# Cross attention's mask moved from a TensorE matmul to a VectorE addition, in a one-core perceiver layer

## The chip, the cores and the metric

The kernel runs on one core of a Trainium2 chip. The metric is the device time of one execution in microseconds; the median of several executions is given. "The profile" is one execution recorded by the hardware profiler, with its trace of every instruction.

## What is computed

One layer on 16 sequences of 64 tokens of 256 numbers: cross attention over a context, self attention, and a mixture of experts, each added to x. The change touches the cross attention only:

```python
# x: (16, 64, 256), ctx: (16, 1601, 256), seg_id: (16, 64), here always 0..127; H=16, HD=128, R=64
kv_c = ctx @ W_kvc ; q_c = layernorm(x) @ W_dq
scores = (q_nope . k_nope + rope(q_rope) . rope(k_rope)) / sqrt(HD + R)
good = (k_ids <= seg_id) & (k_ids >= seg_id - 8)
scores = where(good, scores, -1e30)
attn = softmax(scores)                 # over the context positions
x = x + (attn @ v) @ W_o
x = x + self_attention(layernorm(x))   # 16 heads of 16, causal
x = x + moe(x)                         # 8 experts, top 2, and 2 shared ones
```

A token sees at most nine context positions, all of them within the first 128 where the segment numbers are below 128. So the kernel reads 128 context positions, and has a general path over all 1601 behind a flag that these inputs leave unset.

## The kernel before

The 1024 tokens are 8 tiles of 128, and a tile is two sequences ("blocks" b = 0 and 1) of 64 tokens. Cross attention takes tile after tile: `body(0)`, `body(1)`, a hardware loop over tiles 2 to 6, and `last_body(7)`, which already mixes in the first steps of self attention. Each engine has its own `body`, written out by hand, and semaphores join them. Every `body(i)` also makes the queries and keys of tile i + 1.

The scores of a block are 8 slices of 128 rows (two heads of 64 tokens) by 128 context positions, in two PSUM banks of four slices (banks 4 and 5 for b = 0, 6 and 7 for b = 1). They hold the negated scores, since keys are scaled by a negative number, so softmax takes the minimum.

TensorE, `body` (L1559): transpose of x (`xT`), `scores(i, 0)`, `values(i-1, 1)`, `qc`, `kv`, `y_lat`, `y_rope` of the next tile, `probs_T(i, 0)`, `scores(i, 1)`, `project(i-1)`, `k_T`, `q_T` in two halves (L1359, shown under the helper's line L1320 like every transpose), `values(i, 0)`, `probs_T(i, 1)`. `scores_work` (L1362) begins each bank with one matmul (L1364) that spreads a table of masks over the rows: `sel` picks the row of the block and `win` holds 1e30 where a position is not seen. Four score matmuls (L1368; each f32 matmul runs as two passes in the trace) are summed on top of it.

VectorE, `body` (L698): `maxima(i, 0)` (L643: per bank one `tensor_reduce` from PSUM, L648, then `top_ready`), the copy of the compressed query (L627), `divided(i, 0)` (L652, L653), keys rotated (L603 to L623), `front_rotate` (L609 to L611, which waits for `y_rope`), `maxima(i, 1)`, `front_rotated` (L636, signals `qrope`), `divided(i, 1)`, `front_qt` (L640), the next norm, the residual. In `body(0)` two copies of folded weights (L714) stand behind L636.

ScalarE, `body` (L1152): `exps(i, 0)` (L1097: eight times an exponential of 128x128 with its row sum, each with an accumulator read behind it), `kv_out` (L1086), `kv_raw_out` (L1071 and L1072, signals `kv_raw`, for which `y_rope` waits), `lat_out`, `pt_out` (L1104), `exps(i, 1)`, `k_out` (L1081, signals `kT_done`, for which the second half of `q_T` waits), `qt_hi_out` (L1090), two copies.

GpSimd (L503 to L508) makes `win` [128, 8, 128] once: subtract, square, compare. TensorE waits for it before `body(0)` (L1654). `link` on VectorE and GpSimd makes the engine wait for its own last instruction; in the loop VectorE counts K = 8 such steps per tile.

Of the kernel before, what the change touches and what calls it, by code (L numbers as in the profile page):

```python
# [92 lines left out]
def build(nc, dram):  # L93
    with ExitStack() as ctx:
        def sb(name, shape, dt=F32):
            return ctx.enter_context(nc.sbuf_tensor(name, shape, dt))
# [19 lines left out]
        keypos = packed(consts_a, PACK_A, "keypos")  # L116
        seg_i = sb("seg_i", [P, NT], I32)
        tril = packed(consts_b, PACK_B, "tril")
        hmask = packed(consts_b, PACK_B, "hmask")
        half = sb("half", [P, NT])  # L120
        seg = sb("seg", [P, NT])

# [4 lines left out]
        def carve(store):  # L127
# [102 lines left out]
        xT_all = sb("xT_all", [P, NT, KT, P])  # L230
        b_down = sb("b_down", [P, IC * D])
        b_up = [w_shared[:, 0, 0:GU], x_up[:]]
        b_dn = [w_shared[:, 0, GU:], b_down[:]]
# [49 lines left out]
            yrope_ps yrope_used qrope krope kT_ps kT_done qt_lo_ps qt_lo qt_hi_ps qt_hi kvx  # L283
            s_ps top_ready exp_done p_done pt_ps pt_done ut_ps ut_done proj_ps x2_done ones_set
            bxn bT_ps bxT_done bq_ps bqm bkv_ps bk_done bv_done bs_ps bs_used bmax bsub bp_done bpt_ps
# [7 lines left out]
         yrope_ps, yrope_used, qrope, krope, kT_ps, kT_done, qt_lo_ps, qt_lo, qt_hi_ps, qt_hi, kvx,  # L293
         s_ps, top_ready, exp_done, p_done, pt_ps, pt_done, ut_ps, ut_done, proj_ps, x2_done, ones_set,
         bxn, bT_ps, bxT_done, bq_ps, bqm, bkv_ps, bk_done, bv_done, bs_ps, bs_used, bmax, bsub, bp_done, bpt_ps,
# [37 lines left out]
        def general(eng, tile, first=None, clear=None):  # L333

            eng.wait_ge(far_ready, 1)
            flag = eng.value_load(far_i[0:1, 0:1], min_val=0, max_val=1)
            with eng.If(flag > 0):
                eng.wait_ge(x0_in, 16)
                eng.wait_ge(x_in, 16)
                eng.wait_ge(wv_in, 16)  # L340
                eng.wait_ge(qlat, 1)
                eng.wait_ge(krope, 1)
                eng.wait_ge(qrope, 1)
                eng.wait_ge(win_ready, 1)
# [16 lines left out]
        def _(sp):  # L361
# [114 lines left out]
        def _(pool):  # L476
            steps = [0]

            def link(ins):
                steps[0] += 1  # L480
                ins.then_inc(pool_step, 1)
                pool.wait_ge(pool_step, steps[0])
# [17 lines left out]
            for i in range(2):  # L500
# [3 lines left out]
            pool.wait_ge(seg_moved, 1)  # L504
            link(pool.tensor_tensor(dist, keypos[:].unsqueeze(1).to_broadcast([P, NT, P]),
                                    seg[:].unsqueeze(2).to_broadcast([P, NT, P]), ALU.subtract))
            link(pool.tensor_tensor(dist, dist, dist, ALU.mult))
            pool.tensor_scalar(win[:], dist, (LOOKBACK / 2) ** 2, -NEG, ALU.is_gt, ALU.mult).then_inc(win_ready, 1)  # L508

# [53 lines left out]
        def _(dve):  # L563
# [78 lines left out]

            def maxima(i, b):  # L643
                s = scores_at(b)
                for g in range(2):
                    n = slice(4 * g, 4 * g + 4)
                    dve.wait_ge(s_ps, 2 * TB * i + 2 * b + g + 1)
                    dve.tensor_reduce(neg_top[:, b, n], s[:, n], AX.X, ALU.min).then_inc(top_ready, 1)  # L648

# [35 lines left out]
            def last_body(i, link_):  # L685
                normed(0, 5, xn, bT_ps, bxn, 0)
                maxima(i, 0)
                divided(i, 0, link_)
                b_queries(0)
                maxima(i, 1)  # L690
                normed(1, 7, xn, bT_ps, bxn, 1)
                divided(i, 1, link_)
                residual(i - 1, link_)
                b_maximum(0)
                b_queries(1)
                normed(2, 9, xn, bT_ps, bxn, 2)

            def body(i, link_, behind, more):  # L698
                maxima(i, 0)
                query_compressed(i + 1)  # L700
                if more:
                    link_(dve.bn_stats(bn[:], x_sb[:, i + 2, :]))
                divided(i, 0, link_)
                if more:
                    link_(dve.bn_aggr(mv1[:], bn[:]))
                    dve.tensor_tensor(mv[:, i + 2, :], mv1[:], eps[:], ALU.add).then_inc(mv_ready, 1)
                front_k(i + 1, link_)
                front_rotate(i + 1)
                maxima(i, 1)
# [15 lines left out]
            link(dve.tensor_copy(seg[:], seg_i[:]))  # L725
            dve.tensor_scalar(far[:, 0:NT], seg[:], float(P - 1), None, ALU.is_gt)
            link(dve.tensor_scalar(far[:, NT:2 * NT], seg[:], 0.0, None, ALU.is_lt))
            dve.tensor_reduce(far_n[:], far[:], AX.X, ALU.max).then_inc(flag_set, 1)
# [72 lines left out]
            front_qt(0)  # L801
            dve.wait_ge(x_in, 16)
            body(0, link, False, True)
            body(1, link, True, True)
            base = steps[0]
            K = 8
            with dve.Fori(2, NT - 2) as i:
# [224 lines left out]
        def _(act):  # L1032
# [59 lines left out]
            def exps(i, b, groups=(0, 1)):  # L1092
                s = ps[:, 4 + 2 * b:6 + 2 * b, :].rearrange("p r (h t) -> p (r h) t", t=P)
                for g in groups:
                    act.wait_ge(top_ready, 2 * TB * i + 2 * b + g + 1)
                    for n in range(4 * g, 4 * g + 4):
                        last = act.activation(Pb[:, b, n, :], s[:, n, :], ACT.Exp, scale=-1.0,  # L1097
                                              bias=neg_top[:, b, n:n + 1], accum_out=sums[:, b, n:n + 1])
                    if g:
                        last.then_inc(exp_done, 1)  # L1100
# [217 lines left out]
        def _(pe):  # L1318
# [42 lines left out]

            def scores_work(b, half_, window):  # L1362
                at = ps[:, 4 + 2 * b + half_, :]
                pe.matmul(at.rearrange("p (n k) -> p n k", k=P), sel[:, b, :], window.unsqueeze(1).to_broadcast([P, 4, P]),  # L1364
                          start=True, stop=False)
                for n in range(4):
                    h = 2 * (4 * half_ + n)
                    last = pe.matmul(at[:, n * P:(n + 1) * P], QT[:, b, h:h + 2, :], KTb[:, b, :], start=False, stop=n == 3)  # L1368
                return last
# [560 lines left out]
def laid_out(inputs):  # L1930

    a = {k: np.asarray(v) for k, v in inputs.items()}
    g = lambda n: a["L0_xattn_" + n]
    s = lambda n: a["L0_attn_" + n]
    rows = lambda w: w.reshape(KT, P, -1).transpose(1, 0, 2)
    heads = lambda w, n: w.reshape(n, H, HD).transpose(2, 1, 0)

    def expert(gate, up, down):
# [44 lines left out]
```

## Time and profile before

| what | value |
|---|---|
| median of 3 runs | 513.69 us (513.13 to 515.97) |
| the profiled execution | 514.32 us, of it 512.5 us span |
| TensorE / weight loads busy | 97% / 70% |
| VectorE / ScalarE / GpSimd busy | 48% / 36% / 13% |
| cross attention | from about 23 us to 181 us |

Shares of the whole span mix three stages. The question for this change is what each engine waits for within one tile of cross attention, which the timeline of one tile shows. In the timeline a line has the start, the duration from the first to the last of the merged instructions, and in brackets the idle time before and who ended it. Instructions overlap on an engine: where one follows another without a wait, the distance of two starts (the step) is shorter than the duration.

### The profile page before, as it was taken

How to read it: one execution, taken by the hardware profiler on the slowest of the kernel's cores; microseconds unless marked ns; L12 is line 12 of the kernel's file. 1: busy time of each engine (PE TensorE's matmuls, PEld its weight loads, DVE VectorE, ACT ScalarE, POOL GpSimd, SP SyncE). 2: the span in 40 equal slices, each digit the busy share in tenths (PEclk: the TensorE clock that was granted, in tenths of full speed). 3: DMA queues.
4: the chain of work that ended last, by engine and by line, in shares of the span. 5: the costliest groups of instructions: out<-in, count | busy, mean ns of one | idle time of the engine just before them, and what ended most of it. 6: DMA issues, size and time to landing. Idle time of an engine off the chain costs nothing.

```text
span 512.5 us, 10574 instructions
## 1 busy us (share of the span) xinstructions
PE 496.6 (97%) x3878; PEld 361.1 (70%) x3878; DVE 247.4 (48%) x547; ACT 185.1 (36%) x533; POOL 67.6 (13%) x74
## 2 busy tenths in 40 slices
PE   8799999999999999998999998999999999999997
PEld 7566876876887788886788885555555555556886
DVE  2585776776776678888552221212212222222334
ACT  2267566666667544444411111212212112111110
POOL 6200000000000122232006500000000000000650
PEclk9999999999999999999999999999999999999999
DMA  7830000002990019300704272687877878852341
GB/s 224 300 113 22 0 22 20 0 20 82 369 388 2 2 62 428 128 0 1 277 35 133 73 263 60 262 299 258 313 278 268 321 265 280 306 198 83 86 120 41
DMA packets 24887, 82.05 MB, mean 160 GB/s; under 512 B 2928, under 2 KB 16560, under 8 KB 20880
## 3 DMA queue, kind: packets, MB, share of 16 engines
q1 hardware_dynamic: 21824, 73.30, 39.6%
q0 software_dynamic: 1536, 4.20, 2.6%
q10 hardware_dynamic: 1488, 4.00, 2.1%
q8 instruction: 28, 0.46, 0.3%
q14 instruction: 11, 0.09, 0.1%
HBM read 73.10 MB, written 8.39 MB: 159 GB/s over the span
## 4 chain that ended last, share of the span: by engine, by line
PE 87%; DVE 6%; issue 3%; DMA 1%; ACT 1%; SPq 0%; POOL 0%; DVEq 0%; POOLq 0%
PE ps L1817 17%; PE ps L1725 13%; PE ps L1320 12%; PE ps L1841 9%; PE ps L1737 6%; PE ps L1399 5%; PE ps L1349 5%; PE ps L1368 5%; PE ps L1491 3%; PE ps L1387 3%; DMA w_shared<-in_w_uqk 1%; PE ps L1341 1%; PE ps L1501 1%; PE ps L1681 1%; PE ps L1364 1%
## 5 line engine op out<-in xcount | busy, mean ns | idle before, releaser
L1817 PE MATMUL ps<-w_routed,xnT 128*64 x320 | 93.8, 436 | 1.6 <-DVE x_sb L973 1.6
L1725 PE MATMUL ps<-xT_all,w_shared 128*128 128x256 f32 x320 | 75.6, 380 | 0.0
L1817 PEld LDWEIGHTS ps<-w_routed,xnT 128*64 128x64 f32 x320 | 42.0, 137 | 38.4 <-issue 27.2
L1725 PEld LDWEIGHTS ps<-xT_all,w_shared 128*128 128x128 f32 x320 | 60.3, 190 | 8.4 <-issue 0.4
L1097 ACT ACTIVATE w_routed<-ps,neg_top 128x128 f32<-128x128 f32 x128 | 45.1, 379 | 15.9 <-DVE neg_top L648 15.9
L1841 PE MATMUL ps<-w_routed,hidT 128*64 x200 | 47.4, 384 | 0.0
L1817 PE MATMUL ps<-w_shared,xnT 128*64 128x384 f32 (+1 forms) x160 | 46.9, 436 | 0.0
L1817 PE MATMUL ps<-x_up,xnT 128*64 128x384 f32 (+1 forms) x160 | 46.9, 436 | 0.0
L1320 PEld LDWEIGHTS ps<-consts_a,w_routed 128*128 128x128 f32 x336 | 37.2, 141 | 13.5 <-issue 10.4
L1289 ACT COPY hidT<-ps 128x384 f32<-128x384 f32 x20 | 9.6, 479 | 100.7 <-PE ps L1320 100.7
L1262 ACT ACTIVATE sil<-ps 128x256 f32<-128x256 f32 x40 | 15.4, 384 | 84.3 <-PE ps L1725 84.2
L1320 PE MATMUL ps<-consts_a,w_routed 128*128 128x128 f32 x336 | 44.3, 276 | 1.1 <-DVE w_routed L835 0.5
L1841 PEld LDWEIGHTS ps<-w_routed,hidT 128*64 128x64 f32 x200 | 25.8, 137 | 15.0 <-issue 3.3
L1368 PEld LDWEIGHTS ps<-hid,w_routed 128*128 128x128 f32 x256 | 33.6, 192 | 1.2
L967 DVE COPY hidT<-ps 128x256 f32<-128x256 f32 x20 | 8.5, 425 | 53.4 <-PE ps L1320 53.4
L1368 PE MATMUL ps<-hid,w_routed 128*128 128x128 f32 x256 | 33.7, 275 | 0.0
L558 POOL DMA_INDIRECT x_up<-y_slots,slot_i x8 | 8.0, 997 | 182.7 <-DVE hidT L880 180.5
L648 DVE TENSOR_REDUCE neg_top<-ps 128x4 f32<-128x512 f32 x32 | 22.0, 689 | 16.6 <-PE ps L1368 16.1
L497 POOL TENSOR_TENSOR rstd<-mv,half 128x1 f32 (+1 forms) x16 | 9.1, 567 | 156.8 <-DVE mv L578 95.9
L1349 PE MATMUL ps<-w_routed 96*128 96x512 f32 x64 | 28.9, 593 | 0.3 <-issue 0.3
L1399 PE MATMUL ps<-w_routed 128*128 128x256 f32 x128 | 28.9, 379 | 0.0
L1097 ACT ACTIVATION_READ_ACCUMULATOR w_routed<-ps,neg_top 128x1 f32 x128 | 27.9, 218 | 0.0
(180 smaller groups left out, 873.8 us busy)
## 6 DMA issues: line engine op xcount, KB each, us to landing
w_routed<-in_w_routed SPq DMA_DIRECT2D x8, 1920.0 KB, 14.2
x_up<-in_w_routed SPq DMA_DIRECT2D x10, 1280.0 KB, 5.8
w_shared<-in_w_routed SPq DMA_DIRECT2D x10, 1280.0 KB, 6.1
b_down<-in_w_routed SPq DMA_DIRECT2D x10, 640.0 KB, 5.6
w_shared<-in_w_routed SPq DMA_DIRECT2D x10, 640.0 KB, 5.1
w_shared<-in_w_shared SPq DMA_DIRECT2D x1, 3840.0 KB, 11.8
w_shared<-in_w_uvo ACTq DMA_DIRECT2D x1, 2560.0 KB, 12.7
x_slots<-sil SPq DMA_DIRECT2D x16, 160.0 KB, 2.2
```

Of the source, the lines that this page charges most:

```text
L648: dve.tensor_reduce(neg_top[:, b, n], s[:, n], AX.X, ALU.min).then_inc(top_ready, 1)
L1097: last = act.activation(Pb[:, b, n, :], s[:, n, :], ACT.Exp, scale=-1.0, bias=neg_top[:, b, n:n + 1], accum_out=sums[:, b, n:n + 1])
L1262: act.activation(sil_ring[m % 2], ps[:, UP_BANK[m], 0:D], ACT.Silu).then_inc(up_sil, 1)
L1320: return pe.transpose(out, src, ident[:])
L1349: last = pe.matmul(ps[:, 2 * part + c, :], qcT[:], w[:, c * 512:(c + 1) * 512], start=True, stop=True)
L1368: last = pe.matmul(at[:, n * P:(n + 1) * P], QT[:, b, h:h + 2, :], KTb[:, b, :], start=False, stop=n == 3)
L1387: last = pe.matmul(ps[KVC * h:KVC * h + KVC, 4 + 2 * b, :].rearrange("p (j t) -> p j t", t=P), kv_ext[:, b, 0:KVC], PT[:, b].rearrange("p ...
L1399: last = pe.matmul(ps[:, b, 0:D], UT[:, j, h, :], w_m[:, 2 * j + h, :], start=j == h == 0, stop=j == NP_ // 2 - 1 and h == 1)
L1725: last = pe.matmul(ps[:, UP_BANK[m], half_ * D:(half_ + 1) * D].rearrange("p (n t) -> p n t", n=2), w_shared[:, j, at:at + P], xT_all[:, i ...
L1737: last = pe.matmul(ps[:, Y_BANK[g][n], n * D:(n + 1) * D], hidT_ring[m % 4][:, n * P:(n + 1) * P], w_shared[:, PAIRS[g][0], GU + c * D:GU ...
L1817: last = pe.matmul(ps[rows, b, 0:hi - lo], xnT[:, k, rows], w, start=k == 0, stop=k == KT - 1)
L1841: last = pe.matmul(ps[rows, 6, 0:D], hidT[:, c, rows], w, start=c == 0, stop=c == IC - 1)
```

## The change

The mask is no longer part of the matmul group. Segment numbers come from the host three times side by side: as before, and for each block b its 64 numbers repeated over both halves of the 128 rows. GpSimd makes a table for each block (`spread`, bf16, [128, 2, 8, 128], in the buffer `b_down`), where it made one. VectorE adds the table to a bank of scores, PSUM to SBUF (`Pb`), waits for itself, and takes the minimum from `Pb`. ScalarE takes the exponential of `Pb` in place. TensorE's mask matmuls are gone from the fast path, and each score matmul starts its own slice. VectorE waits for both tables before `body(0)`; TensorE and the SyncE queue no longer wait for `win`.

```diff
+        seg_i = sb("seg_i", [P, (1 + TB) * NT], I32)
+        seg = sb("seg", [P, (1 + TB) * NT])
+        spread = b_down[:, 0:2 * NT * P // 2].bitcast(BF16).rearrange("p (b n t) -> p b n t", b=2, n=NT)
...
@@ sync
-            sp.wait_ge(win_ready, 1)
@@ gpsimd
-            pool.tensor_scalar(win[:], dist, (LOOKBACK / 2) ** 2, -NEG, ALU.is_gt, ALU.mult).then_inc(win_ready, 1)
+            def table(at, out):
+                link(pool.tensor_tensor(dist, keypos[:].unsqueeze(1).to_broadcast([P, NT, P]),
+                                        seg[:, at:at + NT].unsqueeze(2).to_broadcast([P, NT, P]), ALU.subtract))
+                link(pool.tensor_tensor(dist, dist, dist, ALU.mult))
+                return pool.tensor_scalar(out, dist, (LOOKBACK / 2) ** 2, -NEG, ALU.is_gt, ALU.mult)
+
+            for b in range(TB):
+                table((1 + b) * NT, spread[:, b]).then_inc(spread_done, 1)
+                pool.wait_ge(spread_done, b + 1)
@@ vector
-            def maxima(i, b):
+            def maxima(i, b, link_):
                 s = scores_at(b)
                 for g in range(2):
                     n = slice(4 * g, 4 * g + 4)
                     dve.wait_ge(s_ps, 2 * TB * i + 2 * b + g + 1)
-                    dve.tensor_reduce(neg_top[:, b, n], s[:, n], AX.X, ALU.min).then_inc(top_ready, 1)
+                    link_(dve.tensor_tensor(Pb[:, b, n], s[:, n], spread[:, b, i, :].unsqueeze(1).to_broadcast([P, 4, P]), ALU.add))
+                    dve.tensor_reduce(neg_top[:, b, n], Pb[:, b, n], AX.X, ALU.min).then_inc(top_ready, 1)
...
             dve.wait_ge(x_in, 16)
+            dve.wait_ge(spread_done, TB)
             body(0, link, False, True)
             body(1, link, True, True)
             base = steps[0]
-            K = 8
+            K = 12
@@ scalar
-                s = ps[:, 4 + 2 * b:6 + 2 * b, :].rearrange("p r (h t) -> p (r h) t", t=P)
...
-                        last = act.activation(Pb[:, b, n, :], s[:, n, :], ACT.Exp, scale=-1.0,
+                        last = act.activation(Pb[:, b, n, :], Pb[:, b, n, :], ACT.Exp, scale=-1.0,
                                               bias=neg_top[:, b, n:n + 1], accum_out=sums[:, b, n:n + 1])
@@ tensor
-            def scores_work(b, half_, window):
+            def scores_work(b, half_, window=None):
                 at = ps[:, 4 + 2 * b + half_, :]
-                pe.matmul(at.rearrange("p (n k) -> p n k", k=P), sel[:, b, :], window.unsqueeze(1).to_broadcast([P, 4, P]),
-                          start=True, stop=False)
+                if window is not None:
+                    pe.matmul(at.rearrange("p (n k) -> p n k", k=P), sel[:, b, :], window.unsqueeze(1).to_broadcast([P, 4, P]),
+                              start=True, stop=False)
...
-                scores_work(b, 0, win[:, i, :]).then_inc(s_ps, 1)
+                scores_work(b, 0).then_inc(s_ps, 1)
...
-            pe.wait_ge(win_ready, 1)
             body(0, False)
@@ laid_out
-        "seg": a["itok_BxS_0_1023"].reshape(NT, P).T,
+        "seg": np.concatenate([seg] + [np.tile(seg[b * LQ:(b + 1) * LQ], (P // LQ, 1)) for b in range(2)], 1),
```

## Rows read from the trace of the kernel before

**Rows 1.** The page's busy times: us, share of the span, instructions.

```profile
PE 496.6 (97%) x3878; PEld 361.1 (70%) x3878; DVE 247.4 (48%) x547; ACT 185.1 (36%) x533; POOL 67.6 (13%) x74
```

**Rows 2.** Timeline of TensorE, tile 1: start us, us, engine, line, operation.

```profile
42.89 0.38 PE L1364 MATMUL ps<-w_routed,consts_a 128*128 128x512 bf16 x1
43.11 1.05 PE L1368 MATMUL ps<-hid,w_routed 128*128 128x128 f32 x8
44.00 0.38 PE L1364 MATMUL ps<-w_routed,consts_a 128*128 128x512 bf16 x1
...
47.61 3.60 PE L1349 MATMUL ps<-w_routed 96*128 96x512 f32 x8
51.05 1.04 PE L1320 MATMUL ps<-consts_a,w_routed 128*128 128x128 f32 x8
...
57.81 1.91 PE L1320 MATMUL ps<-consts_a,w_routed 128*128 128x128 f32 x16
...
61.81 0.38 PE L1364 MATMUL ps<-w_routed,consts_a 128*128 x1
```

**Rows 3.** Timeline of VectorE, tile 1.

```profile
44.20 0.69 DVE L648 TENSOR_REDUCE neg_top<-ps 128x4 f32<-128x512 f32 x1 [3.67 <-PE ps L1368]
...
51.25 1.23 DVE L609 TENSOR_TENSOR w_routed<-ps,consts_a 128x1024 f32<-128x1024 f32 x1 [0.76 <-PE ps L1349]
...
53.59 1.44 DVE L648 TENSOR_REDUCE neg_top<-ps 128x4 f32<-128x512 f32 x2
54.95 1.21 DVE L636 TENSOR_TENSOR w_routed<-w_routed 128x1024 f32<-128x1024 f32 x1
```

**Rows 4.** Timeline of ScalarE, tile 1.

```profile
44.92 0.37 ACT L1097 ACTIVATE w_routed<-ps,neg_top 128x128 f32<-128x128 f32 x1 [0.77 <-DVE neg_top L648]
...
47.68 0.34 ACT L1086 COPY hidT<-hidT 128x128 f32<-128x128 f32 x1
...
48.29 0.27 ACT L1072 COPY w_routed<-ps 128x128 f32<-128x128 f32 x1
```

**Rows 5.** Groups by shape, 30 to 190 us: count, busy us, mean ns, idle before.

```profile
L610 DVE TENSOR_TENSOR w_routed<-ps,consts_a 128x512 f32<-128x512 f32 x7 | 4.8, 680 | 0.0
L676 DVE TENSOR_REDUCE smx<-w_routed 128x16 f32<-128x1024 f32 x2 | 2.4, 1220 | 0.1
```

**Rows 6.** Timeline of ScalarE: 1024 columns from PSUM, from SBUF, each with its follower.

```profile
42.87 1.01 ACT L1104 COPY w_routed<-ps 128x1024 f32<-128x1024 f32 x1 [0.43 <-PE ps L1320]
43.78 0.38 ACT L1063 COPY xnT<-ps 128x256 f32<-128x256 f32 x1
...
186.99 1.06 ACT L1233 ACTIVATE w_routed<-w_routed 128x1024 f32<-128x1024 f32 x1 [0.33 <-POOL w_routed L528]
187.95 0.74 ACT L1119 COPY w_routed<-ps 64x256 f32<-64x256 f32 x2
```

**Rows 7.** Timeline, tile 0: the first reduction, block 1's exponentials, second half of q_T.

```profile
24.85 0.69 DVE L648 TENSOR_REDUCE neg_top<-ps 128x4 f32<-128x512 f32 x1 [1.77 <-PE ps L1368]
...
34.64 0.37 ACT L1097 ACTIVATE w_routed<-ps,neg_top 128x128 f32<-128x128 f32 x1 [1.17 <-DVE neg_top L648]
...
37.97 1.07 PE L1320 MATMUL ps<-consts_a,w_routed 128*128 128x128 f32 x8 [0.20 <-ACT hid L1081]
```

**Rows 8.** Timeline, tile 7: each block's division by VectorE and its transposes.

```profile
161.68 1.23 DVE L653 TENSOR_TENSOR w_routed<-w_routed,rec 128x1024 f32<-128x1024 f32 x1
162.96 1.09 PE L1320 MATMUL ps<-consts_a,w_routed 128*128 128x128 f32 x8
...
169.10 1.23 DVE L653 TENSOR_TENSOR w_routed<-w_routed,rec 128x1024 f32<-128x1024 f32 x1
...
170.88 1.09 PE L1320 MATMUL ps<-consts_a,w_routed 128*128 128x128 f32 x8
```

**Rows 9.** Timeline of GpSimd while it makes the table.

```profile
7.89 1.90 POOL L505 TENSOR_TENSOR xT_all<-consts_a,seg 128x1024 f32<-128x1024 f32 x1 [1.63 <-DVE seg L729]
...
11.85 3.65 POOL L508 TENSOR_SCALAR w_routed<-xT_all 128x1024 bf16<-128x1024 f32 x1
```

More of the change, by code:

```diff
@@ L116, in build @@
         keypos = packed(consts_a, PACK_A, "keypos")
-        seg_i = sb("seg_i", [P, NT], I32)
+        seg_i = sb("seg_i", [P, (1 + TB) * NT], I32)
         tril = packed(consts_b, PACK_B, "tril")
@@ L120, in build @@
         half = sb("half", [P, NT])
-        seg = sb("seg", [P, NT])
+        seg = sb("seg", [P, (1 + TB) * NT])
         w_shared = sb("w_shared", [P, NSH, WX])
@@ L283, in build @@
             yrope_ps yrope_used qrope krope kT_ps kT_done qt_lo_ps qt_lo qt_hi_ps qt_hi kvx
-            s_ps top_ready exp_done p_done pt_ps pt_done ut_ps ut_done proj_ps x2_done ones_set
+            s_ps top_ready exp_done spread_done p_done pt_ps pt_done ut_ps ut_done proj_ps x2_done ones_set
             bxn bT_ps bxT_done bq_ps bqm bkv_ps bk_done bv_done bs_ps bs_used bmax bsub bp_done bpt_ps
@@ L293, in build @@
          yrope_ps, yrope_used, qrope, krope, kT_ps, kT_done, qt_lo_ps, qt_lo, qt_hi_ps, qt_hi, kvx,
-         s_ps, top_ready, exp_done, p_done, pt_ps, pt_done, ut_ps, ut_done, proj_ps, x2_done, ones_set,
+         s_ps, top_ready, exp_done, spread_done, p_done, pt_ps, pt_done, ut_ps, ut_done, proj_ps, x2_done, ones_set,
          bxn, bT_ps, bxT_done, bq_ps, bqm, bkv_ps, bk_done, bv_done, bs_ps, bs_used, bmax, bsub, bp_done, bpt_ps,
@@ L343, in general @@
                 eng.wait_ge(qrope, 1)
-                eng.wait_ge(win_ready, 1)
+                eng.wait_ge(spread_done, TB)
                 eng.wait_ge(rstd_ready, 2)
@@ L504, in _ @@
             pool.wait_ge(seg_moved, 1)
-            link(pool.tensor_tensor(dist, keypos[:].unsqueeze(1).to_broadcast([P, NT, P]),
-                                    seg[:].unsqueeze(2).to_broadcast([P, NT, P]), ALU.subtract))
-            link(pool.tensor_tensor(dist, dist, dist, ALU.mult))
-            pool.tensor_scalar(win[:], dist, (LOOKBACK / 2) ** 2, -NEG, ALU.is_gt, ALU.mult).then_inc(win_ready, 1)
+            def table(at, out):
[6 more added lines that the diff above has]
+                pool.wait_ge(spread_done, b + 1)
             def g_tile(i):
@@ L686, in last_body @@
                 normed(0, 5, xn, bT_ps, bxn, 0)
-                maxima(i, 0)
+                maxima(i, 0, link_)
                 divided(i, 0, link_)
                 b_queries(0)
-                maxima(i, 1)
+                maxima(i, 1, link_)
                 normed(1, 7, xn, bT_ps, bxn, 1)
@@ L698, in body @@
             def body(i, link_, behind, more):
-                maxima(i, 0)
+                maxima(i, 0, link_)
                 query_compressed(i + 1)
@@ L708, in body @@
                 front_rotate(i + 1)
-                maxima(i, 1)
+                maxima(i, 1, link_)
                 front_rotated(i + 1)
@@ L725, in _ @@
             link(dve.tensor_copy(seg[:], seg_i[:]))
-            dve.tensor_scalar(far[:, 0:NT], seg[:], float(P - 1), None, ALU.is_gt)
-            link(dve.tensor_scalar(far[:, NT:2 * NT], seg[:], 0.0, None, ALU.is_lt))
+            dve.tensor_scalar(far[:, 0:NT], seg[:, 0:NT], float(P - 1), None, ALU.is_gt)
+            link(dve.tensor_scalar(far[:, NT:2 * NT], seg[:, 0:NT], 0.0, None, ALU.is_lt))
             dve.tensor_reduce(far_n[:], far[:], AX.X, ALU.max).then_inc(flag_set, 1)
@@ L1360, in qT_work @@
                 return last
-            def scores_work(b, half_, window):
+            def scores_work(b, half_, window=None):
                 at = ps[:, 4 + 2 * b + half_, :]
-                pe.matmul(at.rearrange("p (n k) -> p n k", k=P), sel[:, b, :], window.unsqueeze(1).to_broadcast([P, 4, P]),
-                          start=True, stop=False)
+                if window is not None:
+                    pe.matmul(at.rearrange("p (n k) -> p n k", k=P), sel[:, b, :], window.unsqueeze(1).to_broadcast([P, 4, P]),
+                              start=True, stop=False)
                 for n in range(4):
                     h = 2 * (4 * half_ + n)
-                    last = pe.matmul(at[:, n * P:(n + 1) * P], QT[:, b, h:h + 2, :], KTb[:, b, :], start=False, stop=n == 3)
+                    last = pe.matmul(at[:, n * P:(n + 1) * P], QT[:, b, h:h + 2, :], KTb[:, b, :], start=window is None,
+                                     stop=window is None or n == 3)
                 return last
@@ L1445, in scores @@
                     after(pe, x2_done, i - 1)
-                scores_work(b, 1, win[:, i, :]).then_inc(s_ps, 1)
+                scores_work(b, 1).then_inc(s_ps, 1)
             def probs_T(i, b):
@@ L1934, in laid_out @@
     s = lambda n: a["L0_attn_" + n]
+    seg = a["itok_BxS_0_1023"].reshape(NT, P).T
     rows = lambda w: w.reshape(KT, P, -1).transpose(1, 0, 2)
```

## The prediction

> **What bounds the kernel now.** I read the busy times first: TensorE is busy for 97% of the span, the others for half of it or less [rows 1]. That is a mean over three stages, so it only says to ask what TensorE waits for inside a tile of cross attention, where all of the change lies. The timeline of one tile answers that, engine by engine. Tile 1 runs from its first mask at 42.89 to that of tile 2 at 61.81, 18.92 us [rows 2], and TensorE hardly pauses. So cutting TensorE's work pays only as far as no other chain of waits is nearly as long. To see that, I follow the semaphores through VectorE and ScalarE [rows 3, 4]: block 0's exponentials gate `kv_raw`, and so `y_rope`; `y_rope` gates the three rotations on VectorE; these stand ahead of block 1's minima and of the second rotation step, which gate both halves of `q_T`.
>
> **What is removed.** A mask matmul holds TensorE from 42.89 to 43.11, 0.22 us, and four score matmuls take the rest of the 1.11 to the next mask, 0.89 [rows 2]. Four per tile are 0.86 to 0.88, and 32 in the kernel 6.9 us. That is the most that the change can give: TensorE alone would need about 18.06 a tile.
>
> **What is added on VectorE.** Per bank one addition of 128x512, PSUM with a table in SBUF, out to SBUF. Its nearest row is L610, the same shape and places but for the table's bf16: 0.68 us [rows 5], and I take that, with 0.64 to 0.72 as bounds. The reduction then waits for it (0.04). The reduction itself changes from PSUM to SBUF; one of 1024 columns from SBUF takes 1.220 [rows 5], an operation of 1024 columns from PSUM 1.23 [rows 3], so it stays at 0.69. A pair of add and reduction occupies VectorE 0.72 + 0.61 = 1.33 where a reduction took 0.61 (the second one at 53.59 had waited for its scores, so two took 1.36 [rows 3]; two pairs take 2.66). Behind them in VectorE's order stand the query copy (block 0) and the second rotation with `qrope` (block 1). In the loop the address of the tile's table must also be computed after the wait for the scores; I put 0.06 on it, an estimate that no row here shows (left out, each of the five tiles of the loop would be that much shorter).
>
> The Trainium skill, VectorE: DVE Perf Modes, section on the TRN2 errata, gives VectorE a fixed term of 58 cycles from SBUF and 120 from PSUM at 0.96 GHz. By that a reduction from `Pb` would be 0.065 shorter, some 0.2 per tile and 1.6 in all off the sum below. The rows just named differ by 0.01 only, and the sum goes by them.
>
> **What is moved on ScalarE.** The 128 exponentials now read SBUF. Today eight take 47.68 - 44.92 = 2.76, 0.345 each with the accumulator read [rows 4]. No row shows one from SBUF. The nearest pair is of 1024 columns: from PSUM 1.01 and the next instruction 0.91 after the start, from SBUF 1.06 and 0.96 [rows 6]. The extra 0.05 is thus in the step and not only in the latency, though the second is an exponential and the first a copy. For 128 columns a copy from SBUF takes 0.34, from PSUM 0.27 [rows 4]. I call the extra per exponential d: bounds 0 (hidden behind the accumulator read) and 0.07; I take 0.045, by the longer pair, a little under for the difference of function.
>
> The same skill page and section gives ScalarE 224 cycles from SBUF and 172 from PSUM at 1.2 GHz and says that the latency is exposed between instructions; d would be 0.043. It speaks against this change; the trace agrees with it at 1024 columns, with 0.05.
>
> **The cycle of a tile after the change**, from one start of `y_rope` to the next, by steps of these rows:
> - `y_rope` is the second half of 3.44 (47.61 to 51.05), 1.72, and 0.20 to VectorE at 51.25 [rows 2, 3].
> - Rotations, 51.25 to 53.59: 2.34 [rows 3].
> - Then two branches to the second half of `q_T`. By `qrope`: two pairs 2.66, second rotation 1.21 [rows 3], 0.13 to TensorE (between the 0.05 of VectorE's division in rows 8 and the 0.15 behind `k_out`; an estimate), first half of `q_T` 0.88: 4.88. By the exponentials: 0.72 + 0.69 + 0.04, eight of them 2.76 + 8d, and 0.57 for `k_out` (in tile 0 34.64 + 2.76 = 37.40, and the second half at 37.97 [rows 7]): 4.78 + 8d.
> - From there to the next tile's scores: 61.81 - 57.81 - 0.88 = 3.12 [rows 2]; scores without mask 0.89; 0.20 to VectorE: 4.21.
> - Address 0.06, add 0.72, reduction 0.69, 0.04 to ScalarE: 1.51.
> - Eight exponentials 2.76 + 8d.
> - From the last of them to the end of L1072: 48.29 + 0.27 - 47.68 = 0.88 [rows 4], and 0.14 to `y_rope`: 1.02.
>
> Sum with d = 0: 1.72 + 0.20 + 2.34 + 4.88 + 4.21 + 1.51 + 2.76 + 1.02 = 18.64, 0.28 less than now. With d = 0.045 the exponentials add 0.36 in the sixth item and, as 4.78 + 0.36 exceeds 4.88 by 0.26, that too: 19.26, 0.34 more than now. TensorE's 18.06 is reached in neither. Six tiles (1 to 6) make -1.7 or +2.0.
>
> **Tile 0** has no slack to start with. Its first reduction starts at 24.85; without the mask the scores are there 0.22 earlier, at 24.63, so exponentials start at 24.63 + 0.72 + 0.69 + 0.04 = 26.08, and `y_rope` at 26.08 + 2.76 + 1.02 = 29.86 (+ 8d). Now it starts at 34.64 - 0.71 (a reduction) - 2.34 - 1.92 = 29.67. The second half of `q_T` follows at 29.86 + 1.92 + 2.34 + 4.88 = 39.00 against 37.97 [rows 7]: +1.03; with d = 0.045, 30.22 + 4.26 + 5.14 = 39.62, +1.65. The copies of L714, moved behind the longer minima, end before the folded matmuls that need them.
>
> **Tile 7.** Block 0's division ends at 161.68 + 1.23 = 162.91 and its transposes start at 162.96: no slack [rows 8]. Exponentials start 0.72 - 0.22 = 0.50 later, so +0.50 (+0.86 with d). Block 1 adds -0.22 + 0.72 (+0.36), and its division ends at 170.33 for transposes at 170.88 [rows 8], about 0.50 of slack: +0.50, or 0.86 + 0.86 - 0.50 = +1.22.
>
> **GpSimd.** A table took from 7.89 to 11.85 + 3.65 = 15.50, 7.61 [rows 9]. The second would end at about 23.2; VectorE wants it at 24.63 [rows 7]. Nothing is queued behind its wait but that first addition, so both tables and the longer load of segment numbers cost nothing with 1.4 to spare; if the cover goes, each further us costs one. The waits for `win` that go from TensorE and SyncE had long been satisfied. The smaller K-steps, the casts of 24 instead of 8 columns and the removed matmuls' addresses are nothing.
>
> **Sum.** d = 0.045: 1.65 + 6 x 0.34 + 1.22 = +4.9. d = 0: 1.03 - 6 x 0.28 + 0.50 = -0.15. d = 0.07: 2.05 + 6 x 0.74 + 1.62 = +8.1. The addition's bounds move each by about 1.0. Behind cross attention every stage and its weight loads are released by its results, so I carry the difference to the end one to one. The profiled execution took 514.32, 0.6 above the median of 513.69; the difference is applied to both: 519.2 in a profile, 518.6 as a median.
>
> **Rivals.**
> - ScalarE's read of SBUF is hidden: d below 0.027, the value at which the sum comes to 2.6. For it: the accumulator read already holds the next instruction back, and a latency could end under it. Against: the steps in rows 6. It gives -0.15, 513.5: not slower.
> - d of 0.06 and more, by the short copies [rows 4]: 521.8 at 0.07.
> - VectorE's pairs are shorter than their rows: only if the cycle falls by 0.6 below 18.64 does TensorE's own 18.06 bound again and the 6.9 come out, 507 at best. It takes d = 0 and 0.2 off each of three pairs; the rows for the shape, 0.68 and 0.69, speak against it. Half of that gives 510.5. The page's fixed terms for VectorE, above, are the mild form of it.
> - The tables come late: GpSimd or VectorE slowed by each other's accesses between 15 and 23 us. At a fifth slower the second ends at 7.89 + 2 x 9.13 = 26.2 [rows 9], and 1.6 is added to the forecast: 520.2.
>
> **Chances.** Forecast (d from 0.027 to 0.06) 0.50; larger d 0.12; tables late 0.04; hidden read 0.27; short pairs 0.07. A measurement of this kernel can tell about 0.5%, 2.6 us, from no change. So slower 0.66, same 0.27, faster 0.07. The range takes in the hidden read with a short addition (512.6) and reaches almost to d = 0.07 (521.5); the forecast's own is 516 to 520.5.
>
> **What would show it.** The exponential's step is the decisive row: 0.345 in a group of eight, or 0.39. Tile to tile 18.64 or 19.26 instead of 18.92. Short waits of TensorE ahead of `y_rope` (0.4 and more) and ahead of `q_T`. Adds of 0.68 each followed by a reduction of 0.69. Tile 0 longer by 1.0 to 1.6. The first addition near 24.6, without waiting for GpSimd. I am wrong if tiles fall to 18.1, or if the first addition starts after 25.

## The result and the profile after

| what | before | after |
|---|---|---|
| median | 514.62 us (513.13 to 515.97, 5 runs) | 520.31 us (519.82 to 520.74, 5 runs) |
| ratio after / before | | 1.011, 95% interval 1.0083 to 1.0137 |
| the profiled execution | 514.32 us, span 512.5 | 520.74 us, span 518.9 |

The kernel became 1.1% slower. The median is 1.7 us above the forecast of 518.6 and inside the range; 0.9 of the 1.7 is the kernel before, whose own median was 513.69 when the forecast was made and is 514.62 here. One of the 18 executions of the kernel before beside the last four experiments took 1290 us and is in no ratio. By the same rows as ahead of the prediction, first the page: busy times, the chain's first line, and the group of the exponentials.

```profile
PE 497.3 (96%) x3846; PEld 357.8 (69%) x3846; DVE 266.5 (51%) x579; ACT 188.1 (36%) x533; POOL 76.0 (15%) x77
...
PE 68%; DVE 14%; ACT 8%; issue 6%; DMA 1%; SPq 1%; DVEq 1%; POOL 0%; ACTq 0%; POOLq 0%
...
L1103 ACT ACTIVATE w_routed<-w_routed,neg_top 128x128 f32<-128x128 f32 x128 | 49.5, 388 | 26.1 <-DVE neg_top L654 26.1
```

The same line of the chain for the kernel before:

```profile
PE 87%; DVE 6%; issue 3%; DMA 1%; ACT 1%; SPq 0%; POOL 0%; DVEq 0%; POOLq 0%
```

TensorE lost its 32 mask matmuls (3878 instructions less 3846) and yet its busy time stands at 497 us [rows 1] (ends of matmuls are modelled, and the clock, last section, lengthened some). The busy line would say that nothing happened. The chain tells: TensorE's share of it fell from 87% to 68%, and VectorE and ScalarE came in.

TensorE's timeline, from the second half of tile 0 to the end of tile 7. It answers to rows 2, 7 and 8 of before; L1326 is the transposes, L1375 the scores, L1355 `y_rope`.

```profile
38.81 2.10 PE L1326 MATMUL ps<-consts_a,w_routed 128*128 128x128 f32 x16 [1.47 <-DVE w_routed L641]
...
44.55 0.38 PE L1326 MATMUL ps<-consts_a,xn 128*128 128x128 f32 x2
44.77 1.95 PE L1375 MATMUL ps<-hid,w_routed 128*128 128x128 f32 x16
...
51.37 1.95 PE L1355 MATMUL ps<-w_routed 96*128 96x512 f32 x4 [0.42 <-ACT w_routed L1079]
...
59.69 2.10 PE L1326 MATMUL ps<-consts_a,w_routed 128*128 128x128 f32 x16
...
63.67 0.38 PE L1326 MATMUL ps<-consts_a,xn 128*128 128x128 f32 x2
...
121.74 0.38 PE L1326 MATMUL ps<-consts_a,xn 128*128 128x128 f32 x2
...
141.14 0.38 PE L1326 MATMUL ps<-consts_a,xn 128*128 128x128 f32 x2
...
164.76 2.05 PE L1499 MATMUL ps<-xnT,w_routed 128*128 128x128 f32 x16 [1.32 <-ACT xnT L1117]
...
176.01 1.09 PE L1326 MATMUL ps<-consts_a,w_routed 128*128 128x128 f32 x8 [0.65 <-DVE w_routed L659]
...
185.98 0.43 PE L1535 MATMUL ps<-hid,w_routed 64*128 64x64 f32 x2
```

The short transposes of x mark the start of a tile. Tile 1 lasts 63.67 - 44.55 = 19.12 us, and tile 5, inside the hardware loop, 141.14 - 121.74 = 19.40; before, every tile lasted 18.92 [rows 2]. Waits stand where TensorE had none: 0.42 ahead of `y_rope` (0.55 in the loop), 1.47 in tile 0 ahead of `q_T`.

ScalarE's timeline, tile 1, answers to rows 4: two exponentials that follow each other, then `kv_out` and the end of `kv_raw_out`.

```profile
47.71 0.39 ACT L1103 ACTIVATE w_routed<-w_routed,neg_top 128x128 f32<-128x128 f32 x1
...
48.09 0.39 ACT L1103 ACTIVATE w_routed<-w_routed,neg_top 128x128 f32<-128x128 f32 x1
...
50.40 0.28 ACT L1093 COPY hidT<-hidT 128x128 f32<-128x128 f32 x1
...
50.95 0.27 ACT L1079 COPY w_routed<-ps 128x128 f32<-128x128 f32 x1
```

The step is 0.385 where it was 0.345: from 47.71 to `kv_out` at 50.40 are seven steps, 2.69. VectorE's timeline, answering to rows 3 and 7: the first addition of tile 0, two pairs in tile 1, and an addition in the loop with the residual's last step (L583) ahead of it.

```profile
24.97 0.69 DVE L653 TENSOR_TENSOR w_routed<-ps,b_down 128x512 f32<-128x512 f32 x1 [1.58 <-PE ps L1375]
...
45.86 0.69 DVE L653 TENSOR_TENSOR w_routed<-ps,b_down 128x512 f32<-128x512 f32 x1 [3.18 <-PE ps L1375]
46.59 0.69 DVE L654 TENSOR_REDUCE neg_top<-w_routed 128x4 f32<-128x512 f32 x1
47.19 0.68 DVE L653 TENSOR_TENSOR w_routed<-ps,b_down 128x512 f32<-128x512 f32 x1
...
122.83 0.16 DVE L583 TENSOR_TENSOR mv<-mv,eps 128x2 f32 x1
123.34 0.69 DVE L653 TENSOR_TENSOR w_routed<-ps,b_down 128x512 f32<-128x512 f32 x1 [0.35 <-PE ps L1375]
```

The span grew by 6.4 us. The starts of tiles share it out: 0.30 ahead of tile 0 (23.53 for 23.23), 1.58 in tile 0 (21.02 for 19.44), 2.19 in tiles 1 to 6 (44.55 to 160.26; before 42.67 to 156.19), 1.06 in tile 7 (from its scores at 160.26 to the first scores of self attention at 185.98, 25.72; before from 156.19 to 180.85, 24.66). The last 1.3 are put down to the clock and not to the change: TensorE's clock fell for a few microseconds near 242 in this execution and not in that of before (the last section), and between two landmarks of the expert stages around it the delay grows by that much: the first matmul of L1732 comes 5.0 us later than before (242.2 for 237.2), that of L1824 6.3 (318.3 for 312.0).

### The profile page after: what moved, and what is told of

Its sections match the earlier page's. It is cut to its first block, busy times and chain, and to the rows that moved or that the text cites. A ratio compares the mean times of both kernels' runs of the same rounds, so it can differ in the third digit from the quotient of the medians.

```text
span 518.9 us, 10565 instructions
## 1 busy us (share of the span) xinstructions
PE 497.3 (96%) x3846; PEld 357.8 (69%) x3846; DVE 266.5 (51%) x579; ACT 188.1 (36%) x533; POOL 76.0 (15%) x77
## 4 chain that ended last, share of the span: by engine, by line
PE 68%; DVE 14%; ACT 8%; issue 6%; DMA 1%; SPq 1%; DVEq 1%; POOL 0%; ACTq 0%; POOLq 0%
PE ps L1824 17%; PE ps L1732 12%; PE ps L1326 9%; PE ps L1848 9%; ACT w_routed L1103 7%; PE ps L1744 6%; PE ps L1355 3%; PE ps L1499 3%; DVE neg_top L654 2%; PE ps L1407 2%; DVE w_routed L653 2%; PE ps L1375 2%; DMA w_routed<-in_ctxT 1%; PE ps L1688 1%; PE ps L1509 1%
## 5 line engine op out<-in xcount | busy, mean ns | idle before, releaser
L1824 PE MATMUL ps<-w_routed,xnT 128*64 x320 | 93.8, 436 | 1.6 <-DVE x_sb L980 1.6
L1732 PE MATMUL ps<-xT_all,w_shared 128*128 128x256 f32 x320 | 77.0, 385 | 0.0
L1824 PEld LDWEIGHTS ps<-w_routed,xnT 128*64 128x64 f32 x320 | 42.0, 137 | 38.4 <-issue 27.2
L1732 PEld LDWEIGHTS ps<-xT_all,w_shared 128*128 128x128 f32 x320 | 61.3, 193 | 8.8 <-issue 0.4
L1103 ACT ACTIVATE w_routed<-w_routed,neg_top 128x128 f32<-128x128 f32 x128 | 49.5, 388 | 26.1 <-DVE neg_top L654 26.1
L1326 PEld LDWEIGHTS ps<-consts_a,w_routed 128*128 128x128 f32 x336 | 38.4, 145 | 18.8 <-issue 14.8
L1326 PE MATMUL ps<-consts_a,w_routed 128*128 128x128 f32 x336 | 47.3, 284 | 3.6 <-DVE w_routed L641 1.5
L1824 PE MATMUL ps<-w_shared,xnT 128*64 128x384 f32 (+1 forms) x160 | 46.9, 436 | 0.0
L1824 PE MATMUL ps<-x_up,xnT 128*64 128x384 f32 (+1 forms) x160 | 46.9, 436 | 0.0
L1355 PE MATMUL ps<-w_routed 96*128 96x512 f32 x64 | 30.9, 608 | 4.8 <-ACT w_routed L1079 3.6
L1375 PE MATMUL ps<-hid,w_routed 128*128 128x128 f32 x256 | 31.2, 275 | 0.0
L1375 PEld LDWEIGHTS ps<-hid,w_routed 128*128 128x128 f32 x256 | 29.9, 192 | 0.0
L986 DVE COPY y_sb<-ps 128x256 f32<-128x256 f32 x20 | 8.5, 425 | 37.5 <-PE ps L1848 37.5
L1407 PEld LDWEIGHTS ps<-w_routed 128*128 128x128 f32 x128 | 23.8, 190 | 2.9
```

Source lines behind the costliest of these rows:

```text
L1103: last = act.activation(Pb[:, b, n, :], Pb[:, b, n, :], ACT.Exp, scale=-1.0, bias=neg_top[:, b, n:n + 1], accum_out=sums[:, b, n:n + 1])
L1326: return pe.transpose(out, src, ident[:])
L1355: last = pe.matmul(ps[:, 2 * part + c, :], qcT[:], w[:, c * 512:(c + 1) * 512], start=True, stop=True)
L1407: last = pe.matmul(ps[:, b, 0:D], UT[:, j, h, :], w_m[:, 2 * j + h, :], start=j == h == 0, stop=j == NP_ // 2 - 1 and h == 1)
L1732: last = pe.matmul(ps[:, UP_BANK[m], half_ * D:(half_ + 1) * D].rearrange("p (n t) -> p n t", n=2), w_shared[:, j, at:at + P], xT_all[:, i ...
L1824: last = pe.matmul(ps[rows, b, 0:hi - lo], xnT[:, k, rows], w, start=k == 0, stop=k == KT - 1)
```

## The experiments

Theory A, of the prediction: the exponential from SBUF takes 0.04 us more, and those steps, on a cycle that joins ScalarE, VectorE and TensorE, make the loss. Theory B: the additions alone make it, wherever their output lies. Lines of code in the diffs are those of the kernel after.

### The sum stays in PSUM

```diff
-link_(dve.tensor_tensor(Pb[:, b, n], s[:, n], spread..., ALU.add))
-dve.tensor_reduce(neg_top[:, b, n], Pb[:, b, n], AX.X, ALU.min)
+link_(dve.tensor_tensor(s[:, n], s[:, n], spread..., ALU.add))
+dve.tensor_reduce(neg_top[:, b, n], s[:, n], AX.X, ALU.min)
-act.activation(Pb[:, b, n, :], Pb[:, b, n, :], ACT.Exp, ...)
+act.activation(Pb[:, b, n, :], s[:, n, :], ACT.Exp, ...)
```

> The changed kernel, but the addition goes back into PSUM, and the minimum and the exponentials read PSUM as before the change. Theory (ScalarE's reads of SBUF cost 0.04 each and lie twice on the cycle of a tile): exponentials step by 0.345 instead of 0.385, a tile takes 18.64 us instead of 19.25, tile 0 still 1.0 longer than before, and the whole is level with the kernel before (ratio 1.000) and 4.3 us under the changed one. Rival (VectorE's additions cost all of it, wherever they write): level with the changed kernel, ratio 1.011. If the dip of TensorE's clock at 20 to 23 us comes with the tables' making, it is here too.

Measured: 515.96 us (515.22 to 517.63, 12 runs) against 514.27 (23 runs), ratio 1.0023, 95% interval 1.0003 to 1.0042. ScalarE's timeline of tile 1:

```profile
47.50 0.36 ACT L1104 ACTIVATE w_routed<-ps,neg_top 128x128 f32<-128x128 f32 x1
...
47.84 0.36 ACT L1104 ACTIVATE w_routed<-ps,neg_top 128x128 f32<-128x128 f32 x1
...
49.89 0.34 ACT L1093 COPY hidT<-hidT 128x128 f32<-128x128 f32 x1
```

The step is back at 0.34 to 0.35, with every addition still there. Tile 1 lasts 18.71, the loop's tiles 18.87, against 19.12 and 19.40. So 4.4 us between the medians (520.31 less 515.96) go with the place of the sum, and this kernel stays 1.7 above the kernel before by the medians, 1.2 by the ratio. (The two don't add up to the 5.7 of the result, because the kernel before was measured again, 514.27 for 514.62.) Theory B's 1.011 is excluded by the interval. What is left lies mostly in tile 0, which has no slack: it lasts 20.61, 1.17 more than before; tiles 1 to 6 together are 0.66 shorter than before, and tile 7 is 0.52 longer. The tiles add up to 1.0.

### No mask at all

This kernel leaves the mask out of the computation: neither matmul nor addition. The tables are still made.

```diff
-link_(dve.tensor_tensor(Pb[:, b, n], s[:, n], spread..., ALU.add))
-dve.tensor_reduce(neg_top[:, b, n], Pb[:, b, n], AX.X, ALU.min)
+dve.tensor_reduce(neg_top[:, b, n], s[:, n], AX.X, ALU.min)
```

(The exponentials read `s`, and K is 8.)

> The changed kernel without any addition of the mask (the output leaves the mask out); minimum and exponentials read PSUM; both tables are still made. It gives what taking the 32 mask matmuls from TensorE is worth by itself. Theory: 18.06 us a tile, 6.2 us under the kernel before, ratio 0.988. Rival (the mask matmuls were hidden behind other waits already): a tile stays near 18.9, ratio 1.000.

Measured: 509.63 us (507.04 to 509.91, 6 runs), ratio 0.9884 (0.985 to 0.9917). TensorE's timeline, the starts of tiles 4 and 5 (98.21 and 116.28):

```profile
98.21 0.38 PE L1326 MATMUL ps<-consts_a,xn 128*128 128x128 f32 x2
...
116.28 0.38 PE L1326 MATMUL ps<-consts_a,xn 128*128 128x128 f32 x2
```

18.07 us: TensorE's own cycle, forecast at 18.06. So the mask matmuls were worth something, of the 6.9 us that their own time adds up to: tiles 1 to 6 together are 5.1 shorter than before (44.01 to 152.41), the medians lie 4.6 apart (514.27 less 509.63), and the ratio, which is not that of the two medians, gives 6.0, between 4.3 and 7.7. That is what the change could have brought had nothing else become late.

### Both kinds of mask

```diff
-scores_work(b, 0)
+scores_work(b, 0, spread[:, b, i, :])
-scores_work(b, 1)
+scores_work(b, 1, spread[:, b, i, :])
```

Each bank gets its matmul back (and the additions stay, so the mask counts twice). In this and the next two kernels TensorE waits for both tables ahead of tile 0.

> The changed kernel with the mask matmuls kept as well (the mask is added twice, which changes nothing in a masked place). Theory: of the four matmuls a tile only the one ahead of block 0's first bank lies on the new cycle, so a tile grows by 0.22 to about 19.4 and the kernel by about 2 us over the changed one. Rival (TensorE still sets the tile): all four count, 0.86 a tile and 6.9 us over the changed one.

Measured: 521.32 us (520.4 to 524.54, 6 runs), ratio 1.0133 (1.0095 to 1.0171); tile 1 lasts 19.36, tiles 3 to 5 last 19.47 to 19.49. Four matmuls of 0.22 a tile, 0.88, cost 0.24 in tile 1 and 0.05 to 0.08 in tiles 3 to 5. So most of them stand in time that TensorE would have waited through. In tile 1 the cost is that of about one, and the one ahead of block 0's first scores is the only one with no wait of TensorE between it and the first reduction; that it is this one which costs is an inference. In the loop it is a third of one, since there VectorE is late for the addition anyway (below). The whole is 1.0 us above the kernel after by the medians, where 2 were expected; the intervals of the two ratios overlap. That is the mirror of the result: taking them out gives nearly nothing while another chain is longer.

### One bank on each engine

TensorE masks the first bank of each block by its matmul, VectorE the second by an addition in PSUM (K is 10, and the exponentials read `s`).

```diff
+if g == 1:
+    link_(dve.tensor_tensor(s[:, n], s[:, n], spread..., ALU.add))
+dve.tensor_reduce(neg_top[:, b, n], s[:, n], AX.X, ALU.min)
-scores_work(b, 0)
+scores_work(b, 0, spread[:, b, i, :])
```

> Split: the first bank of each block is masked by TensorE (from the same tables), the second by VectorE, in place in PSUM. Theory: the second bank's addition hides behind the first bank's exponentials (1.38 us) in both blocks, so the two removed matmuls come out: 18.49 us a tile against 18.92, tile 0 level, 2.7 us under the kernel before, ratio 0.995. Rival (any addition on VectorE delays qrope and costs what the matmul gave): ratio 1.000 or above.

Measured: 512.32 us (511.71 to 515.61, 12 runs), ratio 0.9967 (0.9942 to 0.9992): a little faster than the kernel before, and faster than the kernel after. TensorE's timeline, and VectorE's:

```profile
99.33 0.38 PE L1328 MATMUL ps<-consts_a,xn 128*128 128x128 f32 x2
...
117.82 0.38 PE L1328 MATMUL ps<-consts_a,xn 128*128 128x128 f32 x2
```

```profile
100.85 0.69 DVE L655 TENSOR_REDUCE neg_top<-ps 128x4 f32<-128x512 f32 x1 [1.04 <-PE ps L1377]
101.85 0.70 DVE L654 TENSOR_TENSOR ps<-ps,b_down 128x512 f32<-128x512 f32 x1 [0.31 <-PE ps L1377]
102.59 0.69 DVE L655 TENSOR_REDUCE neg_top<-ps 128x4 f32<-128x512 f32 x1
```

A tile takes 18.49: two mask matmuls less, 0.43, and TensorE bounds again. The first reduction starts as soon as the scores are there, as before, and the second bank's scores come while VectorE reduces the first, so the addition starts in time that VectorE had waited (0.41 in the kernel before, 0.31 still here). Six tiles give 2.6 by this; the medians show 2.0, the ratio 1.7.

### Its mirror image

The first bank by VectorE, the second by TensorE: `if g == 0` in the diff above, and the other call of `scores_work`.

> The mirror image of the split: the first bank of each block is masked by VectorE (in place in PSUM), the second by TensorE. As many additions and as many mask matmuls as in the split of the second banks (0.9967). Theory: an addition ahead of the first bank delays the first exponential, and with it all eight, so it lies on the cycle: about 18.85 us a tile in the loop, tile 0 longer by 0.9, the whole within 0.2% of the kernel before or above (ratio 1.000 to 1.002). Rival (only the number of additions counts, not their place): 18.49 us a tile, ratio 0.997.

Measured: 515.93 us (514.52 to 518.95, 12 runs) against 514.29 (18 runs), ratio 1.003 (1.0008 to 1.0051). The loop's tiles last 18.79 to 18.87, as with all additions in PSUM. Same work on each engine as in the last kernel, 3.6 us apart: it is the first bank's addition, between the scores and the first exponential, that costs.

### VectorE's loop written out

```diff
-with dve.Fori(2, NT - 2) as i:
-    ...
-    body(i, in_loop, True, True)
-steps[0] = base + K * (NT - 4)
+for i in range(2, NT - 2):
+    body(i, link, True, True)
```

With constants for addresses and for the values waited for, nothing is computed between VectorE's instructions.

> The changed kernel with VectorE's hardware loop over tiles 2 to 5 written out, so that no addition and no wait of VectorE needs a register. Theory (a tile in the loop takes 19.40 and one outside 19.12 because VectorE computes addresses and counts between the scores and the addition): all tiles 19.12, 1.1 us under the changed kernel, ratio 1.009. Rival (the 0.28 is the loop of TensorE or ScalarE): tiles 19.40 as before, ratio 1.011.

Measured: 519.09 us (517.94 to 521.09, 6 runs), ratio 1.0093 (1.0067 to 1.0119); every tile from 1 to 5 lasts 19.12. VectorE's timeline at the place shown for the kernel after at 122.83:

```profile
121.96 0.16 DVE L583 TENSOR_TENSOR mv<-mv,eps 128x2 f32<-128x2 f32 x1
122.30 0.69 DVE L653 TENSOR_TENSOR w_routed<-ps,b_down 128x512 f32<-128x512 f32 x1 [0.18 <-PE ps L1365]
```

From the end of L583 to the addition are 0.18 here and 0.35 in the kernel after, and the step from L582 to L583 is 0.21 (121.75 to 121.96) where it is 0.32 (122.51 to 122.83). Together 0.28: all of the difference between 19.12 and 19.40. VectorE's loop covers tiles 2 to 5; the forecast counted five tiles for it, it is four.

### Half of the sums in PSUM, by block

```diff
+to = (s if b == 0 else Pb[:, b])[:, n]
+link_(dve.tensor_tensor(to, s[:, n], spread..., ALU.add))
+dve.tensor_reduce(neg_top[:, b, n], to, AX.X, ALU.min)
```

and the exponentials read the same place; then the same with `b == 1`.

> The changed kernel with block 0 added in place in PSUM and read there; block 1 goes to SBUF as in the change. Theory: block 0's eight exponentials lie on the cycle with all of 8 x 0.04 = 0.32, so 19.08 us a tile in the loop and 18.80 outside. Rival (only the exponentials of block 1 count): 19.40.

> The changed kernel with block 1 added in place in PSUM and read there; block 0 goes to SBUF. Theory: block 1's exponentials lie on the cycle only beyond the 0.1 by which the branch over qrope is longer, so 0.21 comes off: 19.19 us a tile in the loop, 18.91 outside, above the run with block 0 in PSUM. Rival (block 1's exponentials are hidden behind qrope altogether): 19.40.

Measured: block 0 in PSUM 518.36 us (515.81 to 519.07, 6 runs), ratio 1.0071 (1.0045 to 1.0098), tile 1 18.85, in the loop 19.15; block 1 in PSUM 516.95 us (516.21 to 519.21, 7 runs), ratio 1.0057 (1.0033 to 1.008), tile 1 18.98, in the loop 19.13. Each half brings a part, as theory A has it, 0.27 and 0.14 outside the loop for 0.32 and 0.21 expected. Outside the loop their order is the expected one. In the loop it isn't: block 0 is the better half by 0.13 outside and the worse by 0.02 inside. Why is answered by VectorE's queue, below.

## Why the prediction was right, and where a term was not

**The deciding term.** d, the extra step of an exponential from SBUF, was put at 0.045 with bounds 0 and 0.07; it is 0.385 - 0.345 = 0.040. The step taken from the pair of 1024 columns [rows 6] held, and so did the reason: it is the step that grows and not only the latency. The profile shows where: an exponential takes 388 ns where it took 379, and the accumulator read behind it 187 where it took 218, yet the next begins 0.04 later. The Trainium skill, VectorE: DVE Perf Modes, section on the TRN2 errata, gives ScalarE 224 cycles from SBUF for 172 from PSUM at 1.2 GHz, by which d is an estimated 0.043 us; the trace agrees, with 0.040. For VectorE the same section's table has 58 and 120 cycles, by which the reduction from SBUF would be an estimated 0.065 shorter; below the table the section itself says that 58 is too low for a copy that it measured, whose fixed term was about 150. The trace shows no difference: 0.69 from SBUF here and 0.69 from PSUM with the sum in PSUM. The rows were the better guide.

**The addition** takes 0.68 to 0.69, its reduction 0.69, the pair 45.86 to 47.19, 1.33, as forecast.

**The cycle.** With d = 0.04, and without the 0.06 for the address, the forecast's steps give 18.64 - 0.06 + 0.32 + (4.78 + 0.32 - 4.88) = 19.12. Measured outside the loop: 19.12. The exact match owes something to chance. With the sum in PSUM the same steps give 18.58 and tile 1 took 18.71; some of it is `y_rope`, whose second half with the step to VectorE takes 1.99 (51.37 to 53.36) and not 1.92. In return, going to SBUF costs 0.41 a tile (19.12 less 18.71) and not 0.54, for a reason that the forecast doesn't have: the instruction behind the eight exponentials is 0.06 shorter where they read SBUF (`kv_out` 0.28 for 0.34, `k_out` 0.36 at 60.23 for 0.42 at 59.45). Eight exponentials take 3.09 for 2.75, so with that instruction a block costs 0.28 more. Block 0's count in full, 0.27 by the run with block 0 in PSUM (19.12 less 18.85). Block 1's count less what the branch over `qrope` is longer by, forecast at 0.10: with the sum in PSUM the first half of `q_T` ends at 59.27 + 0.88 = 60.15, and `k_out` would release the second at 59.45 + 0.57 = 60.02. That is 0.13, and 0.14 is left by the run with block 1 in PSUM (19.12 less 18.98).

**The mis-sized term: register work in the loop.** "The address of the tile's table must also be computed after the wait for the scores; I put 0.06 on it." The loop costs 0.28 a tile. The forecast's sum has the add start 0.20 after the scores, whatever VectorE did just before, and that is where much of it went. The chain of waits of the kernel after, 119 to 142 us (start us, us, what; DVEq is VectorE's sequencer, L814 the head of its loop):

```profile
122.51 0.18 DVE mv L582
...
122.78 0.05 issue
122.83 0.07 DVE mv L583
122.90 0.03 issue
122.93 0.06 DVEq L814
122.99 0.13 issue
123.12 0.06 DVEq L814
123.19 0.05 issue
123.23 0.06 DVEq L653
123.29 0.05 issue
123.34 0.70 DVE w_routed L653
```

The scores' step is 0.89, so they end at 121.96 + 0.89 = 122.85 (L1375 starts 0.22 after the transposes at 121.74). VectorE ends L583 at 122.99. The chain into the addition comes from VectorE's own queue and not from TensorE. Before, VectorE waited 1.05 us at this point in the loop:

```profile
119.88 0.69 DVE L648 TENSOR_REDUCE neg_top<-ps 128x4 f32<-128x512 f32 x1 [1.05 <-PE ps L1368]
```

The later exponentials of block 1 and the second pair used that up: division (L659), `front_qt` (L645), the next norm (L603) and the residual (L578 to L583) follow each other without a gap. From there 0.14 of lateness, and 0.35 of register work where 0.20 of a plain wait would stand, make an addition 0.49 after the scores. With the sum in PSUM the exponentials are shorter, VectorE ends L583 at 120.77, just as the scores do (119.88 + 0.89), and only the 0.35 stays. VectorE's timeline of that kernel, in the loop:

```profile
120.61 0.16 DVE L583 TENSOR_TENSOR mv<-mv,eps 128x2 f32 x1
121.12 0.70 DVE L653 TENSOR_TENSOR ps<-ps,b_down 128x512 f32<-128x512 f32 x1 [0.35 <-PE ps L1376]
```

There the loop adds 0.16 to a tile (18.87 for 18.71), half of the 0.28. The two mixed kernels follow suit: with block 1's exponentials from SBUF the loop adds 0.30 (19.15 for 18.85), with block 1's from PSUM 0.15 (19.13 for 18.98). Their timelines at the same place agree: with block 0 in PSUM the scores end at 120.37 and L583 at 120.51, and the addition starts at 120.86, 0.49 behind the scores; with block 1 in PSUM the three are 121.57, 121.58 and 121.92, 0.35 behind. That is the reversal that I hadn't expected: block 0's exponentials decide about `y_rope`, block 1's about when VectorE gets to its next addition, and only in the loop, where VectorE's steps are dearer, is the second limit met. How the 0.35 splits between the address and the value waited for is open; no run changed one without the other.

**In the loop and in sum.** The errors nearly cancel (d a little too long, the loop too short): 19.12 outside and 19.40 inside, mean of tiles 1 to 6 (160.26 - 44.55) / 6 = 19.28, forecast 19.26 (tile 7 starts with its scores). So the match of the mean is better than the working deserved.

**Tile 0**: +1.58, forecast +1.65 (1.57 with d = 0.04). **Tile 7**: +1.06, forecast +1.22; the slack of 0.50 ahead of block 1's transposes is gone (a wait of 0.65 at 176.01). **GpSimd**: the second table ended at 23.13 and VectorE's first addition, at 24.97, waited for TensorE. The forecast was 23.2 and 24.6, the rival of late tables was not met. The cover was 1.8, and would have been shorter but for the 0.30 by which TensorE came later.

**The sum.** 1.58 + 2.19 + 1.06 = 4.8 against a forecast of 4.9. The medians lie 5.7 apart, 4.3 to 7.0 by the interval of the ratio, which takes in both. The profiled executions lie 6.4 apart, by the clock. So the mechanism and the size were right. Whether the 0.9 us between 4.8 and 5.7 is chance stays open.

**The rivals.** A hidden read (513.5) falls by the step of 0.385. The kernel with the sum in PSUM, which has d = 0, also shows that this rival was priced too low: +1.7 us in the medians and +1.0 in the tiles for -0.15, by the loop's 18.87 for 18.64 above all. Larger d falls by 0.040, short pairs by 0.69 for each half.

## What to carry to other kernels

Moving work from the busiest engine pays only as far as the next chain is longer than the gap: ask for each moved piece whether it lies between a producer and the first consumer (the first bank: 0.3% slower than before) or in time its new engine waits anyway (the second bank: 0.33% faster than before). A short operation that is repeated many times on a cycle is worth more attention than the one that was moved: here 0.04 us on 128 exponentials made most of the loss, so the place of the sum was more of the price than the sum. In a hardware loop an engine's in-order queue with its register work can become the late one where its waits were the slack; sum its whole queue from the last wait, not only what follows the wait.

## What the runs showed that I had not expected

**The TensorE clock.** The granted clock of the kernel after fell to 0.50, 1.2 of 2.4 GHz, around 21 us and around 243 us. Windows of 2 us: from:to, us, busy of PE, PEld, DVE, ACT and POOL with their counts, PEclk, DMA share, GB/s.

```profile
18.00:20.00 2.00, 0.24 (x2) 0.27 (x3) 1.61 (x2) 0.37 (x1) 1.91 (x2) 0.89 1.06 383
20.00:22.00 2.00, 2.00 (x11) 2.00 (x11) 0.00 (x0) 0.39 (x1) 2.00 (x1) 0.50 1.11 463
22.00:24.00 2.00, 1.95 (x14) 1.74 (x12) 1.22 (x1) 0.48 (x1) 1.13 (x1) 0.75 0.99 399
...
242.00:244.00 2.00, 2.00 (x8) 1.64 (x7) 0.92 (x5) 1.51 (x2) 0.80 (x1) 0.50 0.00 0
```

The same windows of the kernel before:

```profile
18.00:20.00 2.00, 0.00 (x0) 0.00 (x0) 1.87 (x3) 0.95 (x1) 0.00 (x0) 1.00 0.85 290
20.00:22.00 2.00, 1.46 (x14) 1.49 (x15) 0.14 (x1) 0.38 (x1) 0.00 (x0) 1.00 1.06 404
```

The first fall came behind a pause of TensorE from 17.3 to 19.76 us; before, TensorE had the same pause (no matmul from 18 to 20), and its clock stayed at 1.00. Sixteen transposes at 20.21 took 3.27 us, at full clock such sixteen take 1.91 [rows 2]. The making of two tables is not what brings the fall: the kernel with the sum in PSUM has it too (0.50 from 20 to 22 us), but those with both kinds of mask, with the first bank by VectorE and with half of the sums in PSUM make the same tables and stayed at 1.00 from 18 to 24 us. Ahead of the second fall TensorE was busy for 0.41 of the 2 us from 238 to 240. Other executions of the kernel before had a mean clock between 0.989, with 517.2 us, and 0.999, with 512.6, so such falls come and go from one execution to the next of the same program, and differences of 1 or 2 us need many executions.

**GpSimd beside VectorE.** GpSimd's timeline while it makes the second table:

```profile
10.95 3.66 POOL L509 TENSOR_SCALAR b_down<-xT_all 128x1024 bf16<-128x1024 f32 x1
...
18.65 4.48 POOL L509 TENSOR_SCALAR b_down<-xT_all 128x1024 bf16<-128x1024 f32 x1
```

The same compare took 0.82 us more the second time. VectorE's L641, with both inputs in SBUF, took 1.54 at 18.10 us, beside it, and 1.22 everywhere else in this execution. It is not a fixed price: with the sum in PSUM L641 took 1.22 at 18.30, beside a compare of 4.51, and with block 1 in PSUM 1.67 at 18.92, beside one of 3.63. Why one or the other was longer no run here shows. Neither was on the path.
